# A gated cross-attention and expert layer on one core: the first shared block ahead of the last norm's scaling, the next tile's transposes beside the inner unit's, all result additions on VectorE

## The chip, the core and the metric

The kernel runs on one core of a Trainium2 chip. The metric is the device time of one execution in microseconds, median of three runs. The engines named below are TensorE (PE, matmuls; PEld its weight loads), VectorE (DVE), ScalarE (ACT), GpSimd (POOL) and SyncE (SP, here it only issues transfers). Each has its own in-order instruction stream, and semaphores order them against each other.

## The reference, cut to what matters

```python
x = x + tanh(g_xattn) * attention(layernorm(x), ctx, ctx, wq, wk, wv, wo)   # 32 sequences of 64 tokens, width 256
y = layernorm(x)                                # the second norm
probs = softmax(y @ gate_w.T)                   # 8 experts
top_p, top_i = top_k(probs, 2)
out = sum over the two best e: top_p * (silu(y @ fc1[e].T) * (y @ fc2[e].T)) @ proj[e].T    # inner width 176
shared = silu(y @ shared_fc1.T) * (y @ shared_fc2.T) @ shared_proj.T                        # inner width 704
x = x + tanh(g_ffn) * (out + sigmoid(y @ shared_gate_w.T) * shared)
```

All of it is float32. A product of two float32 matrices is made here of three matmuls in a reduced type: each operand is split in a `hi` part (a copy) and a `lo` part (what the copy left out), and hi*hi, lo*hi and hi*lo are accumulated.

## The kernel before, in words

The 2048 tokens are 4 chunks c of 512, each of 4 tiles of 128 tokens. There is no scheduler: for each engine the order of its instructions is the order of the code in its own function, and every dependency is a semaphore (`wait_ge`, `then_inc`). `hi` copies are ScalarE's, `lo` subtractions are VectorE's (helper `sub`, one line for all of them).

The program has four stages.

1. Attention, chunk by chunk. For each tile VectorE adds the residual (`residual(c, j)`, result in the buffer `XB`) and takes the statistics of the second norm (`aggregate(c, p)` for a pair p of tiles), GpSimd makes the rstd (`rstd2(c, p)`), ScalarE scales (`second_apply(c, p)`), TensorE transposes (`second_norm(c, p)`), ScalarE and VectorE evict (`second_hi`, `second_lo`), and the router's matmuls and small VectorE steps (`logits`, `shifted`, `two_best`, `slots`) find each token's experts and its row in the scatter buffer. All of that for chunk c runs inside the attention of chunk c + 1, for the last chunk inside the next stage. SyncE stores `XB` (x2) to HBM.
2. Shared experts for chunks 0 to 2 (`PRE = 3`), in blocks (s, j): chunk s, 128 of the 704 inner columns j. `fc(s, j)` is 12 matmuls into a pair of banks, ScalarE takes the Silu (`s_silu`), VectorE the product (in `s_block`), ScalarE `s_hi`, VectorE the `lo` (line 961, `sh_lo`), and `pj(s, j)` is 12 matmuls that project back. TensorE's order is `pj` of block n - 2, then `fc` of block n (`blocks`). `s_sums(s)` adds the projections of a chunk. Pieces of the expert weights are loaded, copied and split between the blocks, in the order of the table `PIECE_AT`. `route(LAST)` is the last chunk's routing product; VectorE copies its result out of bank 1 (`slots(LAST)`, line 1104, semaphore `v_keep`).
3. A loop over 39 tiles of 128 rows sorted by expert. In step s TensorE multiplies tile s with its expert's first matrices (6 matmuls of 352 columns), transposes the inner unit of tile s - 1 (two transposes, line 716), projects tile s - 2 (5 matmuls of 256 columns) and transposes the rows of tile s + 2 (`xx`, two transposes, line 681). ScalarE and VectorE evict; GpSimd scatters the results to `y2` in HBM; SyncE loads the tiles and, in between, the sums that were stored earlier.
4. Shared experts of chunk 3 (blocks (3, 0) to (3, 5)), while SyncE loads the two results of each token (`Y2[0]`, `Y2[1]`), GpSimd adds the first of them (line 1429) and VectorE the second (`combine(n)`, line 1253; n runs over the chunks 3, 0, 1, 2). Stores end it.

The buffers `XA` and `XB` of attention are the same memory as `STH` (Silu results) and `SHF` (products) of the shared blocks: the first product overwrites `XB` tiles 0 and 1, the second tiles 2 and 3. ScalarE therefore waits for the x2 store and for its own scalings before the first Silu:

```python
second_apply(LAST, 1)
act.wait_ge(d_x2, 16 * N_CH)
act.wait_ge(p_av, 4 * N_CH)
```

## Time and profile before

| | |
|---|---|
| median of 3 runs | 327.76 us (327.75 to 328.55) |
| the profiled execution | 328.36 us, of it 326.6 us span (first to last profiled instruction) |
| TensorE matmuls, weight loads | 285.0 us, 252.2 us busy |
| VectorE, ScalarE, GpSimd | 219.9, 170.6, 116.4 us busy |
| mean granted TensorE clock | 0.969 of full speed |
| HBM traffic | 43.32 MB in transfers, mean 133 GB/s |

A row of a timeline gives the start and the duration in us, engine, line, operation, what it writes and reads (out<-in), the shape, how many were merged, and in brackets how long the engine stood idle before it and what released it. A busy time overlaps the next instruction's: a matmul is shown from its start to its last result, so matmuls that follow each other closely overlap in their rows, and their pace is the distance of their starts. Idle time of an engine that nobody waits for costs nothing.

### The profile page before, as it was taken

Reading aid. Unit: us, or ns where it says so; the run is one execution under the profiler, and the core shown is the slowest. Engines: PE = TensorE matmul, PEld = TensorE weight load, DVE = VectorE, ACT = ScalarE, POOL = GpSimd, SP = SyncE. Lnnn points to the kernel's source line nnn. Section 1 sums busy time; section 2 is a strip of 40 time slices with the busy share of each in tenths; the row PEclk is TensorE's granted clock in tenths of the full one; section 3 lists DMA queues with packets and bytes.
Section 4 is the critical chain, followed back from the end, with each engine's and each line's share of the span. In section 5 each row is a group of like instructions: output and inputs, shape, how many; then the busy total and the mean of one; then the engine's idle time right before and its main releaser. Section 6 shows DMA issues by size and latency. Waiting matters only on the chain.

```text
span 326.6 us, 5834 instructions
## 1 busy us (share of the span) xinstructions
PE 285.0 (87%) x1783; PEld 252.2 (77%) x1783; DVE 219.9 (67%) x694; ACT 170.6 (52%) x399; POOL 116.4 (36%) x146
## 2 busy tenths in 40 slices
PE   0696979989998987797899999899999999999962
PEld 0565959878877765486788887789999999998852
DVE  3655766969868773666466764787777777743684
ACT  1537677777655454355023554456666666644220
POOL 0510351441773416641450000014444444441840
PEclk9999999999999998699799999999999999999985
DMA  6460114211044102533242565344666644314935
GB/s 225 171 194 0 67 49 130 64 48 66 36 135 163 51 19 99 189 136 101 107 151 65 198 206 188 113 134 137 202 203 202 201 139 135 109 67 138 350 125 193
DMA packets 25999, 43.32 MB, mean 133 GB/s; under 512 B 2961, under 2 KB 19601, under 8 KB 25969
## 3 DMA queue, kind: packets, MB, share of 16 engines
q1 hardware_dynamic: 22128, 33.20, 31.8%
q0 software_dynamic: 3408, 9.57, 8.1%
q8 instruction: 15, 0.25, 0.3%
q10 hardware_dynamic: 432, 0.18, 0.3%
q14 instruction: 16, 0.12, 0.1%
HBM read 26.35 MB, written 16.59 MB: 131 GB/s over the span
## 4 chain that ended last, share of the span: by engine, by line
PE 57%; DVE 20%; ACT 10%; issue 6%; DMA 4%; POOL 1%; SPq 0%; DVEq 0%; ACTq 0%; POOLq 0%
PE bank L416 43%; PE bank L639 8%; DVE ew_lo L961 4%; ACT ew_hi L741 4%; PE bank L716 3%; PE bank L681 2%; DVE work L1260 2%; DMA weight_stage<-wa_dram 2%; DVE xt_lo L961 2%; ACT sh_hi L741 2%; DVE neg_max L1001 2%; DMA weight_stage<-ew_dram 1%; ACT xn_all L778 1%; DVE sh_lo L961 1%; ACT work L773 1%
## 5 line engine op out<-in xcount | busy, mean ns | idle before, releaser
L1420 POOL DMA_INDIRECT y_d<-work,dest_of_slot x39 | 37.4, 959 | 88.4 <-ACT work L741 87.2
L416 PE MATMUL bank<-ew_hi,xt_hi 128*128 (+2 forms) x172 | 58.2, 339 | 0.3 <-issue 0.3
L416 PE MATMUL bank<-ew_lo,xt_hi 128*128 (+2 forms) x172 | 51.8, 301 | 0.0
L416 PE MATMUL bank<-ew_hi 128*128 128x256 f32 (+1 forms) x100 | 33.1, 331 | 15.8 <-ACT ew_hi L741 14.1
L961 DVE TENSOR_TENSOR xt_lo<-bank,xt_hi 128x256 fp32r<-128x256 f32 (+2 forms) x90 | 35.7, 398 | 11.6 <-ACT xt_hi L741 11.5
L416 PE MATMUL bank<-ew_hi,xt_lo 128*128 (+1 forms) x133 | 40.6, 305 | 0.0
L416 PE MATMUL bank<-xt_hi,sw_hi 128*128 128x512 f32 x88 | 36.1, 410 | 2.0 <-DVE work L1260 2.0
L741 ACT ACTIVATE xt_hi<-bank 128x256 fp32r<-128x256 f32 (+1 forms) x90 | 36.3, 409 | 2.8 <-PE bank L424 1.6
L416 PE MATMUL bank<-xt_lo,sw_hi 128*128 128x512 f32 x88 | 35.6, 405 | 0.0
L961 DVE TENSOR_TENSOR ew_lo<-bank,ew_hi 128x512 fp32r<-128x512 f32 (+1 forms) x41 | 22.7, 581 | 19.0 <-ACT ew_hi L741 18.9
L416 PE MATMUL bank<-xt_hi,sw_lo 128*128 128x512 f32 x88 | 35.3, 401 | 0.0
L416 PEld LDWEIGHTS bank<-ew_hi 128*128 128x128 f32 x100 | 19.7, 197 | 20.1 <-ACT ew_hi L741 16.5
L1388 POOL DMA_INDIRECT xs_d<-xn_all,slot_of_pair x32 | 31.7, 990 | 10.0 <-issue 7.3
L416 PE MATMUL bank<-ew_lo,ew_hi 128*128 128x256 f32 (+1 forms) x100 | 32.2, 322 | 2.8 <-DVE ew_lo L961 2.3
L416 PEld LDWEIGHTS bank<-ew_hi,xt_hi 128*128 128x128 f32 (+1 forms) x172 | 32.4, 189 | 0.9 <-issue 0.6
L416 PE MATMUL bank<-ew_hi,ew_lo 128*128 128x256 f32 (+1 forms) x100 | 31.9, 319 | 1.2 <-DVE ew_lo L961 1.2
L416 PEld LDWEIGHTS bank<-ew_lo,xt_hi 128*128 128x128 f32 (+1 forms) x172 | 32.7, 190 | 0.1
L639 PE MATMUL bank<-sw_hi,sh_hi 128*128 128x256 f32 (+1 forms) x96 | 28.9, 302 | 4.2 <-DVE work L1104 3.1
L961 DVE TENSOR_TENSOR sh_lo<-work,sh_hi 128x512 fp32r<-128x512 f32 (+1 forms) x24 | 20.2, 840 | 17.1 <-ACT sh_hi L741 17.1
L639 PE MATMUL bank<-sw_hi,sh_lo 128*128 128x256 f32 (+1 forms) x96 | 28.8, 300 | 2.8 <-DVE sh_lo L961 2.8
L897 ACT ACTIVATE work<-bank 128x512 f32<-128x512 f32 (+1 forms) x24 | 14.3, 594 | 30.5 <-PE bank L416 30.5
L1260 DVE TENSOR_TENSOR work<-work,bank 128x512 f32<-128x512 f32 (+1 forms) x24 | 16.5, 687 | 20.0 <-ACT work L897 16.3
(157 smaller groups left out, 705.6 us busy)
## 6 DMA issues: line engine op xcount, KB each, us to landing
work<-xs_d SPq DMA_DIRECT2D x39, 136.0 KB, 2.5
weight_stage<-ew_dram SPq DMA_DIRECT2D x10, 486.5 KB, 4.2
ew_hi<-y_d SPq DMA_DIRECT2D x8, 512.0 KB, 7.9
xn_all<-x_dram SPq DMA_DIRECT2D x4, 512.0 KB, 5.0
work<-ctx_t_dram SPq DMA_DIRECT2D x4, 512.0 KB, 3.4
x_d<-work SPq DMA_DIRECT2D x4, 512.0 KB, 2.9
work<-x_d SPq DMA_DIRECT2D x3, 512.0 KB, 3.3
z_d<-work SPq DMA_DIRECT2D x3, 512.0 KB, 3.5
```

The lines of the kernel that those rows point to most:

```text
L416: last = nc.tensor.matmul(dst, a, b, start=(n == 0), stop=(n == len(pairs) - 1))
L639: last = nc.tensor.matmul(B[4 + t][:, 0:D], SH[a][0:rows, j % 2, t * P:(t + 1) * P], SPJ[b][0:rows, j, :], start=(j == 0 and n == 0), stop ...
L681: last = nc.tensor.transpose(B[w % 2][:, k * P:(k + 1) * P], EX[:, w, k * P:(k + 1) * P], ident)
L716: last = nc.tensor.transpose(B[4 + v][:, i * P:(i + 1) * P], EH[:, v, i * P:(i + 1) * P], ident)
L741: return nc.scalar.activation(dst, src, ACT.Copy, scale=scale)
L773: nc.scalar.activation(XA[:, j, :], XNR[:, c * TPC + j, :], ACT.Identity, bias=nb1[:, j:j + 1], scale=rs1[:, j:j + 1]).then_inc(a_xn, 1)
L897: nc.scalar.activation(STH[0:rows, j % 2, :], B[pair(s, j)][0:rows, :], ACT.Silu).then_inc(a_th, 1)
L961: return nc.vector.tensor_tensor(dst, src, hi.bitcast(F32), ALU.subtract)
L1001: last = nc.vector.tensor_reduce(nmx[r, j % 2:j % 2 + 1], own_keys(B[4 + j % 2], b), mybir.AxisListType.XY, ALU.max, negate=True)
L1260: nc.vector.tensor_tensor(SHF[0:rows, j % 2, :], STH[0:rows, j % 2, :], h2, ALU.mult).then_inc(v_h, 1)
L1388: nc.gpsimd.indirect_dma_start(out=xs_d, out_offset=bass.IndirectOffsetOnAxis(ap=POS[:, i, n:n + 1], axis=0), in_=XN[:, n, :], in_offset=N ...
L1420: nc.gpsimd.indirect_dma_start(out=y2_d, out_offset=bass.IndirectOffsetOnAxis(ap=IX[:, n:n + 1], axis=0), in_=EY[:, n % 4, :], in_offset=N ...
```

## The change

Seven edits in three places.

At the start of the shared stage: on VectorE `two_best(LAST - 1)` moves behind the last `residual` and `aggregate`. On ScalarE `second_apply(LAST, 1)` moves from ahead of the first Silu to behind `s_hi(0, 0)`, and its wait for the x2 store is gone; VectorE's products (0, 0) and (0, 1) wait instead, each for its half of `XB`. The last x2 store is split in two halves with a semaphore each. `second_hi` and `second_lo` of the last chunk move ahead of `s_hi(0, 1)` and of the `lo` of (0, 1). TensorE waits for `v_keep` one block later.

In the loop: TensorE's `xx` transposes move ahead of the projection, and ScalarE's copy of them ahead of its copy of the projection.

At the end: GpSimd's additions are gone, `combine(n)` makes both on VectorE, and it is called one block earlier.

```diff
@@ SyncE
-                sp.wait_ge(v_x2, 4 * c + 4)
-                sp.dma_start(x2_d[c], XB).then_inc(d_x2, 16)
+                if c == LAST:
+                    sp.wait_ge(v_x2, 4 * c + 2)
+                    sp.dma_start(x2_d[c][:, 0:2, :], XB[:, 0:2, :]).then_inc(d_x2, 16)
+                    sp.wait_ge(v_x2, 4 * c + 4)
+                    sp.dma_start(x2_d[c][:, 2:4, :], XB[:, 2:4, :]).then_inc(d_x2_end, 16)
+                else:
+                    sp.wait_ge(v_x2, 4 * c + 4)
+                    sp.dma_start(x2_d[c], XB).then_inc(d_x2, 16)
...
-                if c < PRE:
-                    sp.wait_ge(d_z, 16 * PRE)
+                sp.wait_ge(*((d_z, 16 * PRE) if c < PRE else (d_x2_end, 16)))
@@ TensorE
                         if order[n] == (0, S_BLK - 1):
                             route(LAST)
+                        if order[n] == (1, 0):
                             pe.wait_ge(v_keep, 1)
...
+                if live(s, -2):
+                    n = (m + (1 if u >= 2 else 0)) * 16 + 16
+                    xx(s + 2, (u + 2) % 4, n)
                 if pjs:
...
                     last.then_inc(e_pj, 1)
-                if live(s, -2):
-                    n = (m + (1 if u >= 2 else 0)) * 16 + 16
-                    xx(s + 2, (u + 2) % 4, n)
@@ ScalarE
-            second_apply(LAST, 1)
-            act.wait_ge(d_x2, 16 * N_CH)
             act.wait_ge(p_av, 4 * N_CH)
...
-                    s_hi(s, j)
                     if (s, j) == (0, 1):
                         second_hi(LAST, 0)
                         second_hi(LAST, 1)
+                    s_hi(s, j)
+                    if (s, j) == (0, 0):
+                        second_apply(LAST, 1)
@@ ScalarE, loop: the copy of the xx transposes (EXT) now stands ahead of the copy of the projection (EY)
@@ VectorE
-                if c == LAST:
-                    two_best(LAST - 1)
                 residual(c, 3)
                 aggregate(c, 1)
+            two_best(LAST - 1)
...
-                dve.wait_ge(g_c1, n + 1)
+                dve.wait_ge(d_zl[c], 16)
+                t = slice(c * TPC, (c + 1) * TPC)
+                dve.wait_ge(d_y[0][c], 16)
+                nc.vector.tensor_tensor(XNR[:, t, :], XNR[:, t, :], Y2[0][:, t, :], ALU.add).then_inc(v_y, 1)
+                dve.wait_ge(v_y, n + 1)
                 dve.wait_ge(d_y[1][c], 16)
...
+                if (s, j) == (0, 0):
+                    dve.wait_ge(d_x2, 16 * N_CH)
+                    dve.wait_ge(a_xn2, 4 * LAST + 2)
+                if (s, j) == (0, 1):
+                    dve.wait_ge(d_x2_end, 16)
+                    dve.wait_ge(a_xn2, 4 * N_CH)
...
-                    s_block(s, j)
+                    s_mult(s, j)
+                    if (s, j) == (0, 1):
+                        second_lo(LAST, 0)
+                        second_lo(LAST, 1)
+                    s_lo(s, j)
...
-                    if j >= 3:
-                        combine(j - 3)
+                    if 2 <= j < 5:
+                        combine(j - 2)
@@ GpSimd
-            for c in LAST_FIRST:
-                t = slice(c * TPC, (c + 1) * TPC)
-                pool.wait_ge(d_zl[c], 16)
-                pool.wait_ge(d_y[0][c], 16)
...
-                nc.gpsimd.tensor_tensor(XNR[:, t, :], XNR[:, t, :], Y2[0][:, t, :], ALU.add).then_inc(g_c1, 1)
```

`s_block` is cut in `s_mult` (the product) and `s_lo` (the `lo` part); one is called right behind the other everywhere but in block (0, 1).

The order of ScalarE's instructions at the start of the shared stage, before (L897 is the Silu with the table load ahead of it, L778 the scaling, `sh_hi` is `s_hi`, `xt_hi` is `second_hi`):

```order
L741 ACTIVATE sw_hi<-weight_stage 128x1024 x2
L778 ACTIVATE xn_all<-work,ln_bias,ln_rstd 128x256 x2
L897 ACT_TABLE_LOAD
L897 ACTIVATE work<-bank 128x512
L741 ACTIVATE sh_hi<-work 128x512
L897 ACTIVATE work<-bank 128x512
L741 ACTIVATE sh_hi<-work 128x512
L741 ACTIVATE xt_hi<-bank 128x2x256 x2
L897 ACTIVATE work<-bank 128x512
```

and of the changed kernel (its lines 746, 783 and 900 are 741, 778 and 897 of before):

```order
L746 ACTIVATE sw_hi<-weight_stage 128x1024 x2
L900 ACT_TABLE_LOAD
L900 ACTIVATE work<-bank 128x512
L746 ACTIVATE sh_hi<-work 128x512
L783 ACTIVATE xn_all<-work,ln_bias,ln_rstd 128x256 x2
L900 ACTIVATE work<-bank 128x512
L746 ACTIVATE xt_hi<-bank 128x2x256 x2
L746 ACTIVATE sh_hi<-work 128x512
L900 ACTIVATE work<-bank 128x512
```

The two scalings have moved behind the first Silu and its `hi` copy, the two evictions of the transposes ahead of the second `hi` copy, and the number of table loads is the same.

TensorE's order in one step of the loop, before (L716 the inner unit's transposes, L681 those of `xx`; 352 columns are the expert's first matrices, 256 the projection):

```order
L416 MATMUL bank<-ew_hi,xt_lo 128x352
L716 MATMUL bank<-consts_sb,work 128x128 x2
L416 MATMUL bank<-ew_hi,xt_hi 128x256
L416 MATMUL bank<-ew_lo,xt_hi 128x256
L416 MATMUL bank<-ew_hi,xt_lo 128x256
L416 MATMUL bank<-ew_hi,xt_hi 128x256
L416 MATMUL bank<-ew_lo,xt_hi 128x256
L681 MATMUL bank<-consts_sb,work 128x128 x2
```

and of the changed kernel (L421, L722 and L687 are L416, L716 and L681 of before):

```order
L421 MATMUL bank<-ew_hi,xt_lo 128x352
L722 MATMUL bank<-consts_sb,work 128x128 x2
L687 MATMUL bank<-consts_sb,work 128x128 x2
L421 MATMUL bank<-ew_hi,xt_hi 128x256
L421 MATMUL bank<-ew_lo,xt_hi 128x256
L421 MATMUL bank<-ew_hi,xt_lo 128x256
L421 MATMUL bank<-ew_hi,xt_hi 128x256
L421 MATMUL bank<-ew_lo,xt_hi 128x256
```

The second pair of transposes has moved from behind the projection to ahead of it; nothing was added or taken away.

VectorE's last instructions, before (L1260 the product, L961 `sh_lo`, L1253 the additions of `combine`, L1280 `s_sums`):

```order
L961 TENSOR_TENSOR sh_lo<-work,sh_hi 128x512
L1253 TENSOR_TENSOR xn_all<-xn_all,ew_hi 128x4x256
L1260 TENSOR_TENSOR work<-work,bank 64x512
L961 TENSOR_TENSOR sh_lo<-work,sh_hi 64x512
L1253 TENSOR_TENSOR xn_all<-xn_all,ew_hi 128x4x256
L1280 SCALAR_TENSOR_TENSOR xn_all<-bank,shared_gate,xn_all 128x256 x4
L1253 TENSOR_TENSOR xn_all<-xn_all,ew_hi 128x4x256
```

and of the changed kernel (L1257 and L1260 are the two additions, L1273 the product, L966 `sh_lo`, L1296 `s_sums`):

```order
L966 TENSOR_TENSOR sh_lo<-work,sh_hi 128x512
L1257 TENSOR_TENSOR xn_all<-xn_all,ew_hi 128x4x256
L1260 TENSOR_TENSOR xn_all<-xn_all,ew_hi 128x4x256
L1273 TENSOR_TENSOR work<-work,bank 64x512
L966 TENSOR_TENSOR sh_lo<-work,sh_hi 64x512
L1296 SCALAR_TENSOR_TENSOR xn_all<-bank,shared_gate,xn_all 128x256 x4
L1257 TENSOR_TENSOR xn_all<-xn_all,ew_hi 128x4x256
L1260 TENSOR_TENSOR xn_all<-xn_all,ew_hi 128x4x256
```

The addition that stood behind the last `sh_lo` is a block earlier, and the last pair, behind the sums, has two additions.

## Rows read from the trace of the kernel before

**Rows 1.** The page: busy time of each engine, share of the span, instructions.

```profile
PE 285.0 (87%) x1783; PEld 252.2 (77%) x1783; DVE 219.9 (67%) x694; ACT 170.6 (52%) x399; POOL 116.4 (36%) x146
```

**Rows 2.** Windows: busy PE, PEld, DVE, ACT, POOL, granted clock, DMA share, GB/s.

```profile
129.00:135.80 6.80, 5.49 (x12) 3.79 (x12) 5.12 (x13) 2.55 (x6) 4.39 (x5) 0.50 0.29 98
...
156.30:159.70 3.40, 3.40 (x14) 3.30 (x15) 2.69 (x14) 0.00 (x0) 1.23 (x3) 0.50 0.12 49
```

**Rows 3.** Chain that ended last, 123 to 140: start, us, what.

```profile
123.73 1.09 POOL ln_bias L1350
...
127.16 1.28 ACT L897
128.45 0.61 ACT work L897
...
130.46 0.71 DVE sh_lo L961
...
133.78 0.61 DVE work L1260
...
135.77 1.21 DVE xt_lo L961 x2
...
139.73 3.06 PE bank L639 x24
```

**Rows 4.** TensorE's timeline, 120 to 157.

```profile
120.38 0.39 PE L416 MATMUL bank<-xt_hi,sw_hi 128*128 128x512 f32 x1
...
126.19 0.63 PE L424 MATMUL bank<-consts_sb,xn_all 128*128 128x128 f32 x4
...
129.82 0.79 PE L416 MATMUL bank<-xt_hi,sw_hi 128*128 128x512 f32 x1 [1.97 <-DVE work L1260]
...
134.68 0.63 PE L416 MATMUL bank<-xt_hi,sw_lo 128*128 128x512 f32 x1
...
156.24 0.56 PE L639 MATMUL bank<-sw_hi,sh_hi 128*128 128x256 f32 x1 [3.13 <-DVE work L1104]
```

**Rows 5.** VectorE's timeline in the tail.

```profile
311.72 2.89 DVE L961 TENSOR_TENSOR sh_lo<-work,sh_hi 128x512 fp32r<-128x512 f32 x1 [0.70 <-ACT sh_hi L741]
314.53 1.21 DVE L1253 TENSOR_TENSOR xn_all<-xn_all,ew_hi 128x1024 f32<-128x1024 f32 x1
```

**Rows 6.** GpSimd's timeline in the tail.

```profile
308.37 5.68 POOL L1429 TENSOR_TENSOR xn_all<-xn_all,ew_hi 128x1024 f32<-128x1024 f32 x2 [0.59 <-DMA ew_hi<-y_d]
```

**Rows 7.** Chain that ended last, in the tail.

```profile
317.17 3.23 PE bank L639 x12
```

**Rows 8.** TensorE's timeline, one step of the loop.

```profile
231.60 0.38 PE L681 MATMUL bank<-consts_sb,work 128*128 128x128 f32 x2
231.74 0.41 PE L416 MATMUL bank<-ew_hi,xt_hi 128*128 x1
231.98 0.32 PE L416 MATMUL bank<-ew_lo,xt_hi 128*128 x1
232.14 0.32 PE L416 MATMUL bank<-ew_hi,xt_lo 128*128 x1
...
233.61 0.38 PE L681 MATMUL bank<-consts_sb,work 128*128 128x128 f32 x2
```

**Rows 9.** Chain that ended last, 159 to 169 (L639 is `pj`, L416 here `fc`).

```profile
159.15 3.08 PE bank L416 x12
...
166.81 1.43 PE bank L639 x12
168.24 2.75 PE bank L416 x12
```

**Rows 10.** VectorE's timeline: start of `two_best(2)`, last residual, end of `tile_table(0)`.

```profile
119.66 0.18 DVE L1078 TENSOR_REDUCE work<-work 128x4 f32<-128x32 f32 x1
...
122.45 0.46 DVE L1024 SCALAR_TENSOR_TENSOR work<-bank,softmax_scale,xn_all 128x256 f32<-128x256 f32 x1
...
159.37 0.06 DVE L1140 MEMSET work<- 1x1 f32 x1
```

More of the change, by code:

```diff
@@ L224, in build @@
         d_x = [sem(f"d_xin{c}") for c in range(N_CH)]
-        d_pad = sem("d_pad")
+        d_pad, d_x2_end, v_y = map(sem, ("d_pad", "d_x2_end", "v_y"))
         d_ex = [sem(f"d_ex{i}") for i in range(4)]
@@ L229, in build @@
         d_zl = [sem(f"d_zload{c}") for c in range(N_CH)]
-        g_pay, g_c1, e_ix = map(sem, ("g_payload", "g_c1", "e_ix"))
+        g_pay, e_ix = map(sem, ("g_payload", "e_ix"))
         zeroed, tanh_g, rw_hi, rw_lo = map(sem, ("zeroed", "tanh_g", "rw_hi", "rw_lo"))
@@ L934, in e_step @@
                     copy(EHT[0][:, v, :, :], B[4 + v][:, 0:D].rearrange("p (m n) -> p m n", m=2)).then_inc(e_hh, 1)
+                if live(s, -2):
+                    w = (u + 2) % 2
+                    act.wait_ge(e_xx, s + 3)
+                    at_least(act, e_fc, s + 1)
+                    copy(EXT[0][:, w, :, :], B[w][:, 0:D].rearrange("p (k n) -> p k n", k=KD)).then_inc(e_xh, 1)
                 if live(s, 2):
@@ L939, in e_step @@
                     copy(EY[:, (s - 2) % 4, :], B[6 + u % 2][:, 0:D], scale=WS[:, s - 2:s - 1]).then_inc(e_y, 1)
-                if live(s, -2):
-                    w = (u + 2) % 2
-                    act.wait_ge(e_xx, s + 3)
-                    at_least(act, e_fc, s + 1)
-                    copy(EXT[0][:, w, :, :], B[w][:, 0:D].rearrange("p (k n) -> p k n", k=KD)).then_inc(e_xh, 1)
             act.wait_ge(p_fc, 6 * PRE)
@@ L1249, in combine, with s_mult @@
                 c = LAST_FIRST[n]
-                dve.wait_ge(g_c1, n + 1)
+                dve.wait_ge(d_zl[c], 16)
[3 more added lines that the diff above has]
+                dve.wait_ge(v_y, n + 1)
                 dve.wait_ge(d_y[1][c], 16)
-                t = slice(c * TPC, (c + 1) * TPC)
                 nc.vector.tensor_tensor(XNR[:, t, :], XNR[:, t, :], Y2[1][:, t, :], ALU.add).then_inc(v_c2, 1)
-            def s_block(s, j):
+            def s_mult(s, j):
                 rows = P if j < S_FULL else S_REST
@@ L1259, in s_block, with s_lo @@
                 at_least(dve, v_hl, 6 * s + j - 1)
+                if (s, j) == (0, 0):
[4 more added lines that the diff above has]
+                    dve.wait_ge(a_xn2, 4 * N_CH)
                 nc.vector.tensor_tensor(SHF[0:rows, j % 2, :], STH[0:rows, j % 2, :], h2, ALU.mult).then_inc(v_h, 1)
+            def s_lo(s, j):
+                rows = P if j < S_FULL else S_REST
                 dve.wait_ge(a_hh, 6 * s + j + 1)
@@ L1292, in _ @@
                         shared_tail_lo(1)
-                    if (s, j) == (0, 1):
-                        second_lo(LAST, 0)
-                        second_lo(LAST, 1)
                     if (s, j) == (0, 2):
@@ L1336, in _ @@
                 for j in range(S_BLK):
-                    s_block(s, j)
+                    s_mult(s, j)
+                    s_lo(s, j)
                     if s > PRE and j == 0:
                         s_sums(s - 1)
-                    if j >= 3:
-                        combine(j - 3)
+                    if 2 <= j < 5:
+                        combine(j - 2)
             s_sums(LAST)
@@ L1421, in _ @@
                                              in_=EY[:, n % 4, :], in_offset=None).then_inc(d_ey[n % 4], 16)
-            for c in LAST_FIRST:
-                t = slice(c * TPC, (c + 1) * TPC)
-                pool.wait_ge(d_zl[c], 16)
-                pool.wait_ge(d_y[0][c], 16)
-                if PRE <= c < LAST:
-                    pool.wait_ge(v_z, 4 * c + 4)
-                nc.gpsimd.tensor_tensor(XNR[:, t, :], XNR[:, t, :], Y2[0][:, t, :], ALU.add).then_inc(g_c1, 1)
 def own_keys(bank, b):
```

## Prediction

> **What bounds the kernel now.** I read the page first: TensorE is busy for 285.0 of the 326.6 us of the span [rows 1]. So a microsecond is won only where TensorE waits, where it runs at half clock, or where its instructions take less room. The windows show the granted clock: half of it, 1.2 GHz, in 129.0 to 135.8 and in 156.3 to 159.7 [rows 2], 2.4 GHz around them. The chain of waits then shows who is late in the first of these stretches, and TensorE's own timeline what it lost [rows 3, 4]. Three places matter.
>
> At the hand-over from attention to the feed-forward part TensorE's matmuls of blocks (0,0) and (0,1) end at 126, some transposes follow, and block (0,2) starts at 129.82 after a wait of 1.97 us on the VectorE product of block (0,0). It then runs at half clock until 135.3. The router matmuls wait for the two `second_lo` until 136.98, and `pj(0,0)` starts behind them at 139.7 [rows 3]. In front of the product stand, one behind the other, the statistics of the last token tile (VectorE), the rstd (GpSimd, 123.73), both scalings `second_apply(3,1)`, a table load and the Silu [rows 3].
>
> At 156.24 `pj(0,4)` has waited 3.13 us for the copy L1104 of the routing result, and the next 3.4 us run at half clock [rows 2, 4].
>
> In the tail a `sh_lo` subtraction of VectorE lasts 2.89 us, beside a GpSimd addition L1429, where the same form took 0.71 at 130.46 [rows 3, 5, 6]; then `pj(3,5)` starts at 317.17 and takes 3.23, where `pj(1,0)` took 1.43 [rows 7, 9].
>
> Between 216 and 288 the loop over expert tiles has no TensorE gap: a step is 2.01 us, the distance from the `xx` transposes at 231.60 to those at 233.61 [rows 8]. From 156.24 to 190 there is none either: the chain there is whole TensorE groups, of which [rows 9] show two.
>
> All times below are put on the clock of the trace of before, without the shift already gained.
>
> **Part A, the hand-over.** `two_best(2)` now stands behind the last residual and statistics. These need only the last attention product, whose matmuls stand just ahead of block (0,0)'s first at 120.38 [rows 4]; I put its end 0.15 behind that, 120.5. The residual ran at 122.45 and now runs at 120.55, 1.9 earlier, so GpSimd starts near 121.8 in place of 123.73 and its 2.3 us are over by 124.1 [rows 3, 10]; the rstd is no longer what is waited for. VectorE: residual to the end of the statistics 1.25 (122.45 to about 123.7), `two_best` 2.8 (119.66 to 122.45, it ran straight into the residual [rows 10]), `shared_tail_lo(0)` 1.2 (1024 elements from SBUF, as in the additions of [rows 5]), so it is free at 125.8. ScalarE: block (0,0) ends at 123.3 (twelve matmuls of 0.23 from 120.38, as in the 2.75 of a group of twelve at full clock [rows 9], and the last result 0.17 later), table load 1.28, Silu 0.6 (128.45 to 129.06): 125.2 [rows 3, 4]. The product runs 125.8 to 126.5. Its two other waits are covered: the first half of the x2 store leaves once the residual of tile 1 is done, two residuals earlier, and the scaling of the tiles 0 and 1 is old. The split costs SyncE one more issue, while it has nothing but a wait.
> Then `sh_hi(0,0)` 0.66 (129.78 to 130.46 [rows 3]), to 127.15, and only now the two scalings, 1.1 together: 128.25, where they ended at 127.16, as the table load began. This is the price of the change. Transposes 128.25 to 128.8, and block (0,2) starts at 128.8 and not 129.82, since its bank is long free. VectorE needs 3.93 from `sh_lo(0,0)` to the end of product (0,1) (130.46 to 133.78 + 0.61 [rows 3]): 127.17 + 3.93 = 131.1. The two `second_lo`, now ahead of `sh_lo(0,1)`, take 1.21 more: 132.3, where it was 136.98. Behind the start of the router 2.75 us pass before `pj(0,0)` (136.98 to 139.73), as now.
> What is left is the clock. Full speed throughout: block (0,2) ends at 131.5, the router starts at 132.3, gain 4.7. Clock falling at 129.0 for 6.8 us as now: block (0,2), at 0.43 a matmul (129.82 to 134.68 for eleven, the first slower [rows 4]), ends at 133.9, the router runs at half clock until 135.8, gain about 2.5. Falling for 3.4 us, as in the second stretch, where TensorE worked from its beginning: eight matmuls at 0.43, four at 0.23, end 133.2, gain 3.8. I take 3.8: TensorE still has little but transposes from 126 to 128.8, 2.8 us where it was 3.8, but it works from 128.8 on without a break. The Trainium skill (TensorE: Matmul & The Clock Gate, section PE-mode transpose) says that transposes do not count as work for the clock gate in the way that matmuls do; by it the fall stays, and the sum is the 3.8 or the 2.5, not the 4.7. The trace is in line with it at 129.0, where transposes were most of the work just before.
>
> **Part B, the routing result.** The wait for `v_keep` moves from `pj(0,4)` to behind `fc(1,0)`; only `fc(1,1)` writes that bank. The wait of 3.13 began at 153.1 [rows 4]; `pj(0,4)` can start there, its `sh` halves being older. At full clock it takes 1.43 (`pj(1,0)` in [rows 9]) for 2.91 (156.24 to 159.15), `fc(1,0)` 2.75 for 3.08: it ends at 157.2 in place of 162.23 [rows 9], 5.0 us. The copy, done just before 156.24, is then early by a microsecond. What is late next is VectorE: product (1,0) is queued behind `slots(3)` and `tile_table(0)`, which end at 159.43 [rows 10]. From there product 0.70, `sh_hi` 0.66, `sh_lo` 0.7, and the four sums of `s_sums(0)` of about 0.41 each end near 163.15; `pj(1,0)` is paced by them and ends at 163.5, not at 168.24 (166.81 + 1.43 [rows 9]). Gain 4.7. The cover for slots and table is used up, so a VectorE slower by x there costs x. Everything behind (weight pieces, pads, z stores) is released by this chain, not by an absolute time, so the shift is kept; the scatters of the last chunk are over long before the first tile load asks for them.
>
> **Part C, the loop.** ScalarE and SyncE do the same work per step, in another order. `EXT` is copied 0.6 earlier, `EY` 0.22 later; GpSimd, which sends EY out, idles about half of each step, and a tile load is issued nearly four steps (8 us) ahead of its transposes. For TensorE the question is what a transpose costs beside its neighbour. The first matmul behind two transposes lasts 0.41 and the second starts 0.24 later, against 0.16 further on [rows 8]. That looks like a penalty of 0.08 for each change from transposes to matmuls, and the new order drops one of two per step: 37 x 0.08 = 3.0 us. But that matmul's row starts only 0.14 behind the first of the two transposes, while the row of the pair lasts 0.38, so it overlaps the second one. Four in a row last 0.63 [rows 4]: two more cost 0.25, 0.12 or less for each. Counted through: pair at 231.60, second matmul at 231.98, 0.38 = 2 x 0.11 + 0.16. No penalty is left. The step is 6 x 0.16 + 5 x 0.12 + 4 x 0.11 = 2.0 in either order. I take 0; bounds -3.0 and, if each of two transposes costs 0.125 in a row of four and not 0.11, +1.1.
> The same page of the Trainium skill (TensorE: Matmul & The Clock Gate, section Architectural detail: the array is 16× 32×32, not 1× 128×128) has it that a matmul can begin before its weights are all loaded, which would make the early start a matter of recording; by it the sum is 0, by the bare row it is -3.0.
>
> **Part D, the tail.** The four first additions go from GpSimd (2.8 each in the last two) to VectorE, where this very form takes 1.21 [rows 5, 6]. Three pairs stand behind `sh_lo(3,2)`, (3,3), (3,4). With `sh_lo` back at 0.7: pair 1 ends at 306.5, product (3,3) is 0.3 late, pair 2 at 310.95, product (3,4) 0.6 late, pair 3 from 313.0 to 315.45. Its data are there: GpSimd's addition at 308.37 waited for load 5 of 8 [rows 6], and load 6 needs some 1.5 more. Product (3,5) then starts at 315.45 (was 315.74, behind the addition of 314.53 [rows 5]) and `pj(3,5)` 0.3 earlier too, at 316.85. TensorE is idle from about 314.4 to there, once, where it now also breaks off in the middle of `pj(3,4)` to wait for the `sh_lo` of 2.89. At full clock `pj(3,5)` takes 1.6 to its last result, 3.23 now: sums to 320.05, then both additions of the last pair, 2.42 where one of 1.21 stood: 322.5 against 323.2. The last store follows as now. Gain 0.75; at half clock as now, a loss of 0.85. I take the gain: `pj(3,4)` no longer breaks in its middle.
>
> **Sum.** 3.8 + 4.7 + 0 + 0.75 = 9.25. The profiled execution took 328.36, 0.60 above the median of the runs shown (327.76), and 1.8 above its span. 328.36 - 9.25 = 319.1; against the median 318.5.
>
> **Rivals.**
> (1) The clock gives less: it stays low as long as now in A and `pj(3,5)` runs at half clock. A 2.5, D -0.85: gain 6.35, 321.4. For it: the long stretch of transposes and the 2.4 us idle in the tail. Against it: TensorE resumes sooner. 20 in 100.
> (2) The transposes do cost 0.08 per change: 3.0 more, 315.5. For it the 0.41 rows, against it the count through. 12 in 100.
> (3) Gains A and B are eaten by a wait behind them, most likely the weight pieces: the load of one stands in the chain that ended last. But its issue waits for VectorE's own work on an earlier piece, which moves along. It would leave under 1 us: 327.3, within 0.3%. 4 in 100.
> (4) Slower: in the loop the `xx` transposes now stand ahead of `pj`, so a tile that lands late holds both. It needs tile loads that take over 8 us, or `EY` to bind; it decides from 0.25 per step on (37 x 0.25 = 9.3), which gives 328.7 at 0.28. Nothing in the rows is near it. 3 in 100.
>
> **Numbers.** Forecast as summed, 61 in 100, own range 317.6 to 320.1 (A at 4.7; D at its loss). The range over the cases takes in rival 1 whole and rival 2: 315.4 to 321.8. About 0.3% is what a measurement of this kernel can tell from no change. Faster 0.93, same 0.04 (rival 3), slower 0.03.
>
> **What would show it.** A: router near 132.3 to 134 and `pj(0,0)` near 136 in place of 139.7; `second_apply(3,1)` ending about 1 later than now. B: no TensorE gap before `pj(0,4)`, a short one (0.6) before `pj(1,0)`, no half clock there. C: step still 2.01; 1.93 would prove rival 2. D: every `sh_lo` at 0.7, eight additions of 1.21 on VectorE, `pj(3,5)` at full clock. Wrong if the clock stretches come elsewhere, or if VectorE's queue at 156 to 163 is longer than its rows.

## The result, and the profile after

| | before | changed |
|---|---|---|
| median of 4 runs each, same chip | 328.15 us (327.75 to 331.46) | 317.76 us (317.19 to 319.57) |
| profiled execution, span | 328.36, 326.6 us | 317.83, 316.0 us |

The ratio is 0.9659, 95% interval 0.9613 to 0.9706: faster by 10.4 us by the medians, 9.6 to 12.7 by the interval, where 9.25 were forecast. The page of the changed kernel answers to [rows 1]: TensorE is busy 6.3 us less, VectorE has four instructions more and GpSimd four fewer.

```profile
span 316.0 us, 5837 instructions
PE 278.7 (88%) x1783; PEld 247.6 (78%) x1783; DVE 220.7 (70%) x698; ACT 170.5 (54%) x399; POOL 106.4 (34%) x142
```

Windows of the changed kernel (columns as in [rows 2]): the two stretches at half clock are gone. The tail still has one, as before.

```profile
126.90:131.80 4.90, 4.16 (x21) 2.96 (x19) 4.27 (x9) 2.20 (x5) 3.83 (x5) 1.00 0.51 161
146.60:150.00 3.40, 3.40 (x23) 3.09 (x23) 2.60 (x5) 0.91 (x2) 0.00 (x0) 1.00 0.47 130
303.00:308.70 5.70, 3.10 (x13) 2.50 (x12) 2.38 (x4) 0.63 (x1) 0.00 (x0) 0.74 0.26 92
```

The chain that ended last, from the last residual over the hand-over to block (1,0)'s projection (L1029 is the residual, L1083 to L1100 is `two_best(2)`, `sw_lo` the lo parts of the last shared weights, L1273 the product, `xt_lo` is `second_lo`; it answers to [rows 3, 9]):

```profile
119.17 0.49 DVE work L1029
...
122.47 0.21 DVE work L1097
...
123.09 1.20 DVE sw_lo L966
124.29 0.61 DVE work L1273
...
127.66 1.22 DVE sw_lo L966
128.88 0.60 DVE work L1273
129.48 1.21 DVE xt_lo L966 x2
...
130.73 1.62 PE bank L421 x6
...
133.43 3.07 PE bank L644 x24
...
152.71 2.97 PE bank L421 x12
155.67 0.12 issue
155.79 1.70 PE bank L644 x12
```

No rstd, no table load and no scaling stands in it any more: it is VectorE's own queue from the last residual to the router, but for one `sh_hi` of ScalarE. The wait of 3.13 us of [rows 4] is gone.

One thing has to be taken out first. In the profiled execution of before the early matmuls of 512 columns start 0.43 apart until 19.6, in that of the changed kernel 0.23 apart from 17.0 on. TensorE's timeline of before, then of the changed kernel:

```profile
18.69 0.63 PE L416 MATMUL bank<-ew_hi,ew_lo 128*128 128x512 f32 x1
19.12 0.63 PE L416 MATMUL bank<-ew_hi 128*128 128x512 f32 x1
19.55 0.50 PE L416 MATMUL bank<-ew_lo,ew_hi 128*128 128x512 f32 x1
```

```profile
17.25 0.40 PE L421 MATMUL bank<-ew_hi 128*128 128x512 f32 x1
17.48 0.39 PE L421 MATMUL bank<-ew_lo,ew_hi 128*128 128x512 f32 x1
17.71 0.40 PE L421 MATMUL bank<-ew_hi,ew_lo 128*128 128x512 f32 x1
```

Nothing of the change lies there. The first matmul of block (0,0) is at 120.38 in the one and 118.97 in the other, so 1.41 us of the 10.54 between the two spans is where the clock came up. All stretches are therefore measured from that matmul. In the table each number is the difference of two starts (or ends) in one kernel's TensorE timeline: from block (0,0)'s first matmul to the router's first, to `pj(0,0)`, to `pj(0,4)`, to `pj(1,1)` (the second projection behind the moved wait); then, from the last of the inner unit's transposes (L716 or its like), to `pj(3,5)`, how long that takes to its last result, and to the end of the span. Part A is the hand-over, B the wait for `v_keep`, C the order of the loop, D the additions in the tail.

| kernel | router | pj(0,0) | pj(0,4) | pj(1,1) | to pj(3,5) | it takes | to the end |
|---|---|---|---|---|---|---|---|
| before | 16.64 | 19.28 | 35.86 | 50.45 | 26.11 | 3.22 | 35.50 |
| changed | 11.76 | 14.38 | 27.70 | 41.13 | 25.58 | 3.22 | 36.23 |
| B alone | 16.64 | 20.67 | 35.98 | 49.38 | 25.87 | 3.21 | 35.25 |
| A alone | 11.75 | 14.37 | 30.96 | 44.00 | 26.06 | 3.22 | 35.45 |
| changed without D | 11.74 | 14.37 | 27.68 | 41.07 | 25.86 | 2.17 | 34.18 |
| tail order | 11.76 | 14.39 | 27.71 | 40.85 | 23.48 | 2.16 | 33.95 |
| two_best back | 11.46 | 14.08 | 27.40 | 40.80 | 25.56 | 2.17 | 35.17 |
| scaling back | 12.51 | 16.36 | 29.68 | 43.06 | 25.56 | 3.21 | 36.19 |
| tail and splits | 10.56 | 13.47 | 26.75 | 40.14 | 23.46 | 2.17 | 33.94 |

Before and changed: 9.32 us by `pj(1,1)` (parts A and B), 0.54 from there to the last inner unit (120.24 against 119.70; the traces of runs 3 to 12 have 119.2 to 121.5 there), minus 0.73 in the tail; with the 1.41 of the start that is the 10.54.

### The profile page after: what moved, and what is told of

It reads as the page before. It is cut to its first block, busy times and chain, and to the rows that moved or that the text cites. A ratio compares the mean times of both kernels' runs of the same rounds, so it can differ in the third digit from the quotient of the medians.

```text
span 316.0 us, 5837 instructions
## 1 busy us (share of the span) xinstructions
PE 278.7 (88%) x1783; PEld 247.6 (78%) x1783; DVE 220.7 (70%) x698; ACT 170.5 (54%) x399; POOL 106.4 (34%) x142
## 4 chain that ended last, share of the span: by engine, by line
PE 56%; DVE 23%; ACT 9%; issue 6%; DMA 4%; POOL 1%; SPq 0%; DVEq 0%; ACTq 0%
PE bank L421 42%; PE bank L644 7%; DVE ew_lo L966 5%; ACT ew_hi L746 4%; PE bank L722 3%; PE bank L687 3%; DVE work L1273 2%; DMA weight_stage<-wa_dram 2%; DVE xt_lo L966 2%; ACT sh_hi L746 2%; DVE neg_max L1006 2%; DVE xn_all L1257 2%; DMA weight_stage<-ew_dram 1%; DVE sw_lo L966 1%; ACT work L778 1%
## 5 line engine op out<-in xcount | busy, mean ns | idle before, releaser
L421 PE MATMUL bank<-ew_hi,xt_hi 128*128 (+2 forms) x172 | 53.8, 322 | 0.3 <-issue 0.3
L421 PE MATMUL bank<-ew_lo,xt_hi 128*128 (+2 forms) x172 | 51.8, 301 | 0.0
L421 PE MATMUL bank<-ew_hi 128*128 128x256 f32 (+1 forms) x100 | 32.3, 323 | 15.7 <-ACT ew_hi L746 13.9
L421 PE MATMUL bank<-ew_hi,xt_lo 128*128 (+1 forms) x133 | 40.5, 305 | 0.0
L966 DVE TENSOR_TENSOR xt_lo<-bank,xt_hi 128x256 fp32r<-128x256 f32 (+2 forms) x90 | 35.6, 397 | 2.7 <-ACT xt_hi L746 1.5
L1406 POOL DMA_INDIRECT xs_d<-xn_all,slot_of_pair x32 | 33.3, 1040 | 10.3 <-issue 7.0
L966 DVE TENSOR_TENSOR ew_lo<-bank,ew_hi 128x512 fp32r<-128x512 f32 (+1 forms) x41 | 22.6, 581 | 19.1 <-ACT ew_hi L746 19.0
L421 PEld LDWEIGHTS bank<-ew_hi 128*128 128x128 f32 x100 | 19.3, 193 | 19.9 <-ACT ew_hi L746 16.4
L421 PE MATMUL bank<-xt_hi,sw_hi 128*128 128x512 f32 x88 | 34.8, 396 | 0.0
L421 PE MATMUL bank<-xt_lo,sw_hi 128*128 128x512 f32 x88 | 34.5, 392 | 0.0
L421 PE MATMUL bank<-xt_hi,sw_lo 128*128 128x512 f32 x88 | 34.4, 391 | 0.0
L421 PE MATMUL bank<-ew_lo,ew_hi 128*128 128x256 f32 (+1 forms) x100 | 31.6, 316 | 3.0 <-DVE ew_lo L966 2.5
L746 ACT ACTIVATE xt_hi<-bank 128x256 fp32r<-128x256 f32 (+1 forms) x90 | 32.7, 409 | 2.8 <-PE bank L429 1.6
L421 PEld LDWEIGHTS bank<-ew_hi,xt_hi 128*128 128x128 f32 (+1 forms) x172 | 32.4, 188 | 0.9 <-issue 0.6
L421 PEld LDWEIGHTS bank<-ew_lo,xt_hi 128*128 128x128 f32 (+1 forms) x172 | 32.7, 190 | 0.1
L421 PE MATMUL bank<-ew_hi,ew_lo 128*128 128x256 f32 (+1 forms) x100 | 31.5, 315 | 1.2 <-DVE ew_lo L966 1.2
L746 ACT ACTIVATE sh_hi<-work 128x512 fp32r<-128x512 f32 (+1 forms) x24 | 15.2, 632 | 27.1 <-DVE work L1273 25.0
L966 DVE TENSOR_TENSOR sh_lo<-work,sh_hi 128x512 fp32r<-128x512 f32 (+1 forms) x24 | 16.6, 691 | 16.5 <-ACT sh_hi L746 16.5
L746 ACT ACTIVATE ew_hi<-bank 128x512 fp32r<-128x512 f32 (+1 forms) x45 | 21.6, 517 | 11.9 <-PE bank L421 6.2
```

Of the source, the lines that this page charges most:

```text
L421: last = nc.tensor.matmul(dst, a, b, start=(n == 0), stop=(n == len(pairs) - 1))
L746: return nc.scalar.activation(dst, src, ACT.Copy, scale=scale)
L966: return nc.vector.tensor_tensor(dst, src, hi.bitcast(F32), ALU.subtract)
L1406: nc.gpsimd.indirect_dma_start(out=xs_d, out_offset=bass.IndirectOffsetOnAxis(ap=POS[:, i, n:n + 1], axis=0), in_=XN[:, n, :], in_offset=N ...
```

## The experiments

Each kernel was timed beside the kernel before on the same chip. The kernel before had medians of 329.75, 331.01 and 330.37 us in the three sets (11 to 17 runs each, 326.6 to 334.0); a ratio is good to about 0.5%, so what is smaller is read from the traces.

**1. Part B alone.**

```diff
                         if order[n] == (0, S_BLK - 1):
                             route(LAST)
+                        if order[n] == (1, 0):
                             pe.wait_ge(v_keep, 1)
```

> The kernel before with part B alone (TensorE's wait for v_keep one block later). Theory: the 3.13 us wait and the half clock behind it go, 4.7 us less than before, ratio 0.986, and the windows show full clock at 156 to 160 (the half clock at 129 to 136 stays). Rival: VectorE's slots and tile table behind the copy, or the clock, give it back: 1.5 us or less, ratio 0.995 or more.

326.19 us (323.24 to 327.80), ratio 0.9905 (0.9861 to 0.9948): 3.1 us less, between the two. The place did as expected: the windows have full clock there. But at the hand-over, whose code is that of before, half clock lasts 10.2 us and not 6.8 as in [rows 2], and lies on the router and the first projections:

```profile
136.00:146.10 10.10, 7.85 (x31) 6.26 (x32) 3.47 (x9) 4.73 (x9) 5.23 (x7) 0.50 0.57 207
153.00:160.00 7.00, 7.00 (x46) 6.36 (x46) 4.67 (x7) 3.29 (x5) 0.00 (x0) 1.00 0.40 105
```

Block (0,2) ran at full clock this time and TensorE then waited 4.18 us for the router's operand. With the same code at the hand-over, how long the clock stays low and which work pays for it differs between executions.

**2. Part A alone** (all edits of the hand-over, none of the others).

```diff
+                if c == LAST:
+                    sp.wait_ge(v_x2, 4 * c + 2)
+                    sp.dma_start(x2_d[c][:, 0:2, :], XB[:, 0:2, :]).then_inc(d_x2, 16)
...
-            second_apply(LAST, 1)
-            act.wait_ge(d_x2, 16 * N_CH)
...
+                    if (s, j) == (0, 0):
+                        second_apply(LAST, 1)
...
+            two_best(LAST - 1)
```

> The kernel before with part A alone (the hand-over: two_best, second_apply, split store, second_hi and second_lo). Theory from the trace of the changed kernel: 4.8 us less, ratio 0.985, with full clock over blocks (0,1) and (0,2). The forecast's value was 3.8 (ratio 0.988) with half clock for 3.4 us. Rival: the gain needs part B too, since the clock falls at the next wait: 2.5 or less, 0.992.

322.45 us (320.40 to 324.60), ratio 0.9809 (0.9737 to 0.9880): 6.3 us less, more than either, though the interval (4.0 to 8.7 us) takes in the 4.8. In the trace the router is 4.89 earlier than in before, the whole hand-over at full clock. The wait for `v_keep` is still there, and the clock does not fall at it (TensorE's timeline, then a window):

```profile
149.74 0.38 PE L644 MATMUL bank<-sw_hi,sh_hi 128*128 128x256 f32 x1 [3.12 <-DVE work L1109]
```

```profile
146.00:153.00 7.00, 3.88 (x27) 3.49 (x26) 5.27 (x18) 1.30 (x3) 1.21 (x2) 1.00 0.34 112
```

**3. The changed kernel without part D** (GpSimd's additions back, `combine` a block later).

> The changed kernel with part D undone: GpSimd makes the first additions again, combine one block later as before. By the trace of the changed kernel D costs 0.6 us (one more 1.23 us addition at the end, product (3,5) 0.6 earlier): this kernel is 0.6 us faster than the changed one, 317.2. By the forecast D gains 0.75: this kernel takes 318.5.

317.48 us (316.06 to 318.80), ratio 0.9643 (0.9581 to 0.9705). The times don't separate it from the changed kernel. The table does, if rows of the same clock are compared. With `pj(3,5)` at half clock the tail takes 35.25 to 35.50 with the old additions (before, A alone, B alone) and 36.2 with the new (changed, scaling back): D costs 0.7 to 1.0. At full clock it is 34.18 against 35.17 (two_best back): 1.0. VectorE's and GpSimd's timelines of this kernel:

```profile
299.09 3.43 DVE L1257 TENSOR_TENSOR xn_all<-xn_all,ew_hi 128x1024 f32<-128x1024 f32 x1
302.44 0.67 DVE L1270 TENSOR_TENSOR work<-work,bank 128x512 f32<-128x512 f32 x1
303.81 1.50 DVE L966 TENSOR_TENSOR sh_lo<-work,sh_hi 128x512 fp32r<-128x512 f32 x1 [0.70 <-ACT sh_hi L746]
305.24 1.21 DVE L1257 TENSOR_TENSOR xn_all<-xn_all,ew_hi 128x1024 f32<-128x1024 f32 x1
```

```profile
298.95 2.48 POOL L1444 TENSOR_TENSOR xn_all<-xn_all,ew_hi 128x1024 f32<-128x1024 f32 x1 [0.61 <-DMA ew_hi<-y_d]
301.96 2.80 POOL L1444 TENSOR_TENSOR xn_all<-xn_all,ew_hi 128x1024 f32<-128x1024 f32 x1 [0.53 <-DMA ew_hi<-y_d]
```

VectorE's instructions with both inputs in SBUF (1.21 and 0.7 alone) stretch to 3.43 and 1.50 beside GpSimd's; the product, which reads a PSUM bank, keeps its 0.67. The Trainium skill (SBUF — State Buffer, section Who interferes with whom) says just this: a VectorE instruction with two SBUF inputs contends with a GpSimd instruction that reads SBUF. The trace agrees.

**4. The changed kernel without part C** (`xx` behind the projection again, and ScalarE's copy of it behind that of the projection).

> The changed kernel with part C undone: xx transposes behind the projection again. Forecast: no change, 317.8, step 2.01 us. By the trace of the changed kernel, whose steps are 2.00 us apart where they were 2.007, C gains 0.3 us: 318.1. Rival 2 (0.08 us for each change from transposes to matmuls): 3.0 slower, 320.8, step 2.08.

319.21 us (316.99 to 320.21), ratio 0.9693 (0.9631 to 0.9754). Its step, by TensorE's timeline:

```profile
230.76 0.38 PE L687 MATMUL bank<-consts_sb,work 128*128 128x128 f32 x2
...
232.77 0.38 PE L687 MATMUL bank<-consts_sb,work 128*128 128x128 f32 x2
```

and the changed kernel's:

```profile
229.92 0.38 PE L687 MATMUL bank<-consts_sb,work 128*128 128x128 f32 x2
231.92 0.38 PE L687 MATMUL bank<-consts_sb,work 128*128 128x128 f32 x2
...
233.92 0.38 PE L687 MATMUL bank<-consts_sb,work 128*128 128x128 f32 x2
```

2.007 to 2.008 against 2.000: 0.3 us over the loop. Not every trace with the new order has that: the last 32 steps take 64.24 us in all four with the old one (before, runs 1, 2 and 4), 64.00 in the changed kernel and runs 7 and 12, 64.11 to 64.24 in runs 3, 5, 6, 8 and 10, and 64.7 and 64.8 in runs 9 and 11. Rival 2 (3.0 us) is out. This execution also had a stretch of half clock from 104.8 to 108.2, in attention, long before the loop: its block (0,0) starts 1.79 later than the changed kernel's, its span is 1.5 longer.

```profile
104.90:108.10 3.20, 3.20 (x17) 3.20 (x17) 2.88 (x13) 0.91 (x4) 0.00 (x0) 0.50 0.00 0
```

**5. The changed kernel again.**

> The changed kernel itself, beside the three that follow: the same time as on record, 317.8, within the scatter of its runs. Both theories expect the phase of the clock's stretches to differ from run to run (full clock from 15 to 20 us on), which alone moves the span by up to 1.4 us.

317.66 us (317.22 to 319.21), ratio 0.9627 (0.9581 to 0.9674). Block (0,0) starts at 119.12, and its tail is 36.20, as in the first. Over the profiles of all kernels that share the start, that block's start lies between 118.47 and 120.93.

**6. Another order in the tail.**

```diff
-                    if 2 <= j < 5:
-                        combine(j - 2)
+                    if j in (2, 3, 5):
+                        combine((2, 3, 5).index(j))
```

> The changed kernel with the third pair of additions behind the lo part of block (3,5) in place of that of (3,4). Theory: the pair stood ahead of product (3,5) and made TensorE idle for 2.3 us; now product (3,5) starts near 301.9, pj(3,5) near 303.2 with hardly a gap ahead of it and at full clock, and VectorE's last work ends 2.1 us earlier: 315.7, ratio to the changed kernel 0.993. Rival: the tail is bound by VectorE's total, and the additions only move: 0.3 or less gained.

315.98 us (315.27 to 319.72), ratio 0.9593 (0.9536 to 0.9649), 1.7 less than the changed kernel of the same set by the medians, with intervals that overlap; in the trace the tail is 33.95 and not 36.23, 2.3 less. `pj(3,5)` starts 0.23 behind `pj(3,4)` where it had waited 2.32, and runs at full clock (TensorE, this kernel, then the changed one):

```profile
303.33 0.38 PE L644 MATMUL bank<-sw_hi,sh_hi 64*128 64x256 f32 x1 [0.23 <-ACT sh_hi L746]
```

```profile
305.38 0.38 PE L644 MATMUL bank<-sw_hi,sh_hi 64*128 64x256 f32 x1 [2.32 <-ACT sh_hi L746]
```

In the changed kernel VectorE's timeline has the third pair of additions right ahead of product (3,5), L1273:

```profile
302.71 1.23 DVE L1260 TENSOR_TENSOR xn_all<-xn_all,ew_hi 128x1024 f32<-128x1024 f32 x1
303.97 0.69 DVE L1273 TENSOR_TENSOR work<-work,bank 64x512 f32<-64x512 f32 x1
```

VectorE's total is the same in both; what counts is which of its work stands ahead of a product that TensorE waits for.

**7 and 8. Work without a use in TensorE's idle 2.3 us.** Ahead of `pj(3,5)`, one of:

```diff
+                        for i in range(10):
+                            nc.tensor.matmul(B[0][:], SFC[0][:, 0, 0, :], XT[0][:, LAST, 0, :], start=True, stop=True)
```

```diff
+                        for i in range(18):
+                            nc.tensor.transpose(B[0][:, 0:P], ident, ident)
```

> The changed kernel with ten matmuls of 512 columns, whose result nobody reads, in TensorE's idle 2.3 us ahead of pj(3,5). Theory (the clock falls because TensorE idles there): pj(3,5) runs at full clock, 1.6 us in place of 3.2, ratio 0.995. Rival (the clock falls there at a set time or from the load before, whatever stands in the gap): no gain.

> The changed kernel with eighteen transposes of 128 columns in the same place, about 2.3 us. By the rule that transposes do not count as work for the clock (the Trainium skill, TensorE: Matmul & The Clock Gate, section PE-mode transpose) pj(3,5) stays at half clock and the time at 317.8. Rival: transposes count like matmuls, the profile shows pj(3,5) at full clock and the time is 1.5 less, as with the ten matmuls.

318.06 us (315.91 to 319.02), ratio 0.9636 (0.9590 to 0.9681), and 318.54 us (316.16 to 318.76), ratio 0.9637 (0.9592 to 0.9682): no gain in either. Both profiled executions have `pj(3,5)` at full clock (2.17 us), but so has run 9, with nothing in the gap, and the three tails take the same (35.15 to 35.17). These two profiles can't carry the theory, and the times show nothing of the 1.5 us. Full clock there is worth 1.05 us (3.22 against 2.17), not 1.6. Whether transposes count for the clock stays open.

**9. two_best(2) back ahead of the last residual.**

> The changed kernel with two_best of chunk 2 ahead of the last residual again, as before. The forecast rests part A on this move (the rstd is no longer waited for). Theory by the trace of the changed kernel: VectorE has the same work ahead of product (0,0) in either order, and with the last scaling behind the first Silu the rstd has until 125.4; no change, 317.7, product (0,0) at the same place, rstd 1.9 later. Rival (the forecast's reason): the last transposes and the router come about 1.9 later, 319.6.

318.08 us (316.33 to 322.57), ratio 0.9646 (0.9595 to 0.9697): no change. The rstd is ready 2.5 us later than in the changed kernel (its last step ends at 124.35 in GpSimd's timeline, 121.89 there), still before the scaling, which now stands behind `sh_hi(0,0)`; the router comes 0.3 earlier, since VectorE no longer idles 0.83 us ahead of the last residual, but 0.56 ahead of product (0,0).

```profile
124.16 0.19 POOL L1374 TENSOR_TENSOR ln_bias<-ln_bias,ln_rstd 128x2 f32<-128x2 f32 x1
```

**10. second_apply(3,1) back ahead of the first Silu.**

> The changed kernel with second_apply(3,1) ahead of the first Silu again (without the wait for the x2 store). Theory: with two_best moved the rstd is done at 121.9, both scalings, table load and Silu end 1.0 later than in the changed kernel (124.9), product (0,0) 0.7 later and the router with it: 318.4. Rival: the scaling is what held the first Silu before, so most of part A's gain goes: 3 us, 320.7.

321.70 us (321.10 to 326.12), ratio 0.9759 (0.9716 to 0.9803): 4 us slower than the changed kernel of run 5, more than the rival's 3, though the theory's chain is right. Product (0,0) (VectorE's timeline) and the router (12.51 against 11.76) are 0.75 later, as worked out.

```profile
125.08 0.69 DVE L1272 TENSOR_TENSOR work<-work,bank 128x512 f32<-128x512 f32 x1 [0.67 <-issue]
```

But the transposes and block (0,2) are earlier, and TensorE stands idle 2.80 us ahead of the router, which then runs at half clock. TensorE's timeline, then a window:

```profile
131.61 0.70 PE L421 MATMUL bank<-xt_hi,router_hi 128*72 128x512 f32 x1 [2.80 <-DVE xt_lo L965]
132.11 0.63 PE L421 MATMUL bank<-xt_lo,router_hi 128*72 128x512 f32 x1
```

```profile
131.40:134.80 3.40, 2.83 (x6) 1.26 (x6) 0.76 (x2) 0.42 (x2) 2.79 (x3) 0.50 0.98 341
```

That makes 1.98 at `pj(0,0)`. A further 1.4 is lost behind block (2,0), where the chain runs through the load of a weight piece: 5.79 us here, 4.43 in the changed kernel. That this belongs to the edit is not shown, for the same load took 3.78 in run 5, the changed kernel again.

**11. The tail of run 6, and both lo parts of the last shared weights behind block (0,1)'s.**

```diff
-            shared_tail_lo(0)
...
                         slots(LAST - 1)
-                        shared_tail_lo(1)
+                    if (s, j) == (0, 1):
+                        shared_tail_lo(0)
+                        shared_tail_lo(1)
```

> The changed kernel with the third pair of additions behind the last lo part (as in the run before) and both lo parts of the last shared weights behind block (0,1)'s lo part, where VectorE waits for the router anyway, in place of ahead of the products (0,0) and (0,1). Theory: 1.6 for the tail and 1.0 at the hand-over (product (0,0) 0.3 earlier, the router 1.2 earlier, pj(0,0) then waits 0.2 for the weights): 315.1, ratio to the changed kernel 0.992. Rival: the hand-over's part is eaten behind the router by VectorE's later weights: 316.1, no better than the tail alone.

316.98 us (314.74 to 319.43), ratio 0.9610 (0.9556 to 0.9663), no better than the tail alone (0.9593), as the rival had it. The router is 1.20 earlier, `pj(0,0)` 0.91, `pj(1,1)` 0.99, as worked out. By the end of chunk 2's blocks nothing is left of it in this execution: the chain has a load of a weight piece of 5.41 us, where the changed kernel's took 4.43, and in the loop a tile load that TensorE waits for (the chains):

```profile
184.87 5.41 DMA weight_stage<-ew_dram
...
219.83 5.96 DMA work<-xs_d
225.83 0.44 PE bank L687 x2
```

**12. The same with work on TensorE from the first microsecond.**

```diff
+            nc.gpsimd.memset(WARM[:], 0.0).then_inc(g_warm, 1)
...
+            pe.wait_ge(g_warm, 1)
+            for i in range(10):
+                nc.tensor.matmul(B[7][:, 0:D], WARM[:, 0:P], WARM[:], start=True, stop=True)
```

> The kernel of the run before it, with ten matmuls of 256 columns in float32 on a zeroed tile, whose result nobody reads, on TensorE from about 1 us to about 9 us, when its first real matmul starts (10.05). Theory (the clock rises once TensorE has worked; so far at 14 to 20 us, 4 to 10 us behind its first matmul): full clock by 10 us and the early chain, 2.7 and 1.7 us of matmuls and transposes at half clock, shorter by 1.5 to 2.2: 313.2, and less scatter. Rival: the clock rises from its own phase, or the start is bound by the load of the weights (6.6 us) and the other engines: 0.5 or less, 314.8.

314.42 us (313.02 to 315.27), ratio 0.9543 (0.9505 to 0.9581): the fastest here, 2.6 less than run 11 by the medians (the two intervals just overlap; the 313.2 expected counted from 315.1 for run 11), and the narrowest of its set. The chains of this kernel and of run 11 at the start (L425 and L421 are the first products, L433 and L429 the transposes of the first tiles):

```profile
11.04 1.56 PE bank L425 x11
12.60 0.45 PE bank L433 x4
...
17.94 3.07 PE bank L425 x12
```

```profile
10.97 2.72 PE bank L421 x11
13.68 1.72 PE bank L429 x8
```

## Why the prediction was right, and where it was not

**The sum.** Of the 9.25 us forecast, 9.1 came in the profiled pair (10.54 less the start's 1.41). The median 317.76 lies 0.7 under the forecast of 318.5. That the sum is so close is in part luck: the terms are off by more (A 1.1 too small, D 1.5 too large), and cancel.

**A, 3.8 forecast, 4.9 measured.** The steps on VectorE, ScalarE and TensorE held: counted from block (0,0)'s start, product (0,0) was forecast at 5.4 and is at 5.24, the end of the scalings at 7.9 and 7.55, the router at full clock at 11.9 and 11.76. The step that failed is the value taken for the clock at the hand-over ("I take 3.8", half clock for 3.4 us): it did not fall. In none of the eleven traces with the Silu ahead of the scaling is a half clock between 110 and 290 us; in before, B alone and run 10, the three in which the scaling stands ahead of the Silu, there is one at the hand-over each time. Alone, A is worth more still: 6.3 us by the times, 6.45 by the trace at `pj(1,1)` (50.45 - 44.00), for in that execution the clock did not fall at the wait for `v_keep` either. The rule on transposes that the forecast weighed led to the wrong side here; the sum of 4.7 without it was the better.

The forecast also gave the gain to one edit of A too narrowly. It rested on `two_best` ("the rstd is no longer what is waited for") and entered the scaling's move as "the price of the change". The runs show two edits that can stand in for each other on the chain: product (0,0) is 8.7 behind block (0,0)'s start in before, 5.98 with `two_best` moved and the scaling left in front (run 10), 4.94 with the scaling moved and `two_best` left (run 9), 5.24 with both. So the first move does what the forecast says, but gains nothing once the scaling stands behind the Silu, and the scaling's move is no price: without it 0.75 is lost on the chain, 1.98 at `pj(0,0)` and 4 us in the times. The remaining 1.4 at the router is the third edit, `second_lo` ahead of the `lo` of block (0,1): the two `second_lo` start 0.6 us behind product (0,1) and not 2.0 (129.48 - 128.88; 135.77 - 133.78 in [rows 3]). The forecast had counted it; no run tests it alone.

**B, 4.7 forecast, 4.4 measured on top of A's 4.90** (9.32 - 4.90). The gap ahead of `pj(1,0)` is a chain piece of 0.12, not 0.6. But the parts are not simply additive: in the profile of A alone the clock did not fall at the wait of 3.12, and B then adds 2.9 (44.00 - 41.13). Alone it gained 1.07 in its trace (50.45 - 49.38) and 3.1 in the times, for the hand-over was slower there.

**C, 0 forecast, 0.3 at most measured**, inside the bounds; the count of each matmul held. What the forecast entered as nowhere near is there in small: with `xx` first, in run 9 and run 11 a tile load made two steps longer, by 0.2 to 0.5 us each, and none did in the four traces with the old order. Loads of 5.74 and 5.96 us did it, where the forecast asked for over 8. Rival 4's mechanism exists, far below 0.25 for every step.

**D, gain 0.75 forecast, loss 0.7 to 1.0 measured.** The failed step is "I take the gain: `pj(3,4)` no longer breaks in its middle". It hardly breaks (0.15 us and not 1.95), but the third pair of additions stands ahead of product (3,5), TensorE waits 2.32 us, and `pj(3,5)` takes 3.22 as before. `pj(3,5)` starts 0.3 to 0.5 earlier (0.3 forecast), and the second addition of 1.23 at the end outweighs that. Two things were wrong in the gain. The clock there does not follow the order of the additions: `pj(3,5)` runs at half clock in three of the four traces with the old additions and in three of the five with the new ones whose gap was left as it is. And full clock is worth 1.05, where the sum had 1.6 (3.23 less 1.6): even run 9, which has it, ends only 0.33 sooner than before. The alternative in the text, a loss of 0.85, had the right size.

**Rivals.** 1 (the clock gives less) held for the tail and was wrong for the hand-over; 2 is out by the steps of run 4, 4 by the result itself; 3 took nothing in the changed kernel, but in run 11 the smaller gain was eaten on the way, in one execution by a longer load.

**Open.** Why filled gaps (runs 7 and 8) do not shorten the times, and what decides whether the clock falls. Idle time alone does not: at the router it fell with TensorE's wait of 2.80 us (run 10), at `v_keep` it did not with 3.12 (run 2), and ahead of `pj(3,5)` waits of 2.32 have both. What is measured over many executions is that the kernel before has a lower mean granted clock (0.955 to 0.970 in the 11 runs beside run 5) than the changed one (0.983 to 0.988 in its 6).

## What to carry to other kernels

When an engine's order is changed, ask not only when the last operand comes, but also how long TensorE then stands idle in one piece: work that is ready earlier can make the gap longer, and in run 10 0.75 us on the chain came with 1.98 at `pj(0,0)` and 4 us in the times. Additions that fit in an engine's idle time still cost if they stand ahead of the one instruction that TensorE waits for; put them behind it. Two edits that free the same chain do not add up: undo each alone before one is called the cause. Compare traces from a common landmark, after the stretch in which the clock comes up, before a difference is given to an edit.

## What the runs showed of the hardware

**When the clock comes up.** TensorE's first real matmul is at 10.05 to 10.29 us in every trace, and in the thirteen without the added matmuls full clock comes anywhere from 13.7 to 20.0. With float32 matmuls on a zeroed tile from 1.09 us on it was there by 6.8. Against run 11, whose trace is one of the two in which it came last, 11 matmuls of the chain took 1.56 and not 2.72, the eight transposes 1.04 and not 1.91 in TensorE's timeline, and the first matmul of 512 columns started at 14.21 and not 16.08. The Trainium skill (TensorE: Matmul & The Clock Gate, section What's actually happening) says that the moment differs from run to run for the same kernel; the traces agree. It counts the loss as under 1% of a typical span; here the cure was worth 2.6 of 317 us by the medians, 0.8%.

TensorE's timeline of run 12 (the ten added matmuls are twenty records):

```profile
1.09 7.38 PE L418 MATMUL bank<-warm 128*128 128x256 f32 x20 [1.09 <-POOL warm L1371]
10.25 0.38 PE L425 MATMUL bank<-ew_hi 128*128 128x256 f32 x1 [1.78 <-ACT ew_hi L750]
```

**Reading it.** The windows view gives 1.00 for the time before the first change of the clock, also where matmuls of 512 columns are 0.43 apart; there the pace of the starts tells the clock, not the column.
